# A two-layer graph network on one core: PSUM groups are seeded from SBUF by ScalarE, and the identity's term of panels 2 to 7 moves from TensorE to VectorE

## What is computed

```python
# layer 0
d = rsqrt(sum(adj, axis=1) + 1e-6)
h0 = (d[:, None] * (adj + eye(N)) * d[None, :]) @ (x @ W0)
x1 = layernorm(x + h0)
# layer 1
msg = relu((adj @ x1) @ W_msg.T + b_msg)
out = layernorm(x1 + gru_cell(msg, x1, W_ih, W_hh, b_ih, b_hh))
```

## Time and profile before

| | us |
|---|---|
| median of 3 runs (range) | 1829.5 (1828.28 to 1831.34) |
| the profiled execution, device time | 1829.18 |
| its span in the trace | 1827.4 |
| PE busy | 1677.5 (92%) |
| DVE busy | 1467.0 (80%) |
| ACT busy | 662.3 (36%) |
| POOL busy | 138.0 (8%) |
| mean granted TensorE clock | 0.992 |

### The profile page before, as it was taken

One profiled execution on the slowest core, in us unless ns is written; L12 is line 12 of the kernel. 1 busy time (PEld: TensorE's weight loads), 2 busy tenths in 40 slices (PEclk: granted clock), 3 DMA queues, 4 the chain that ended last, 5 costly groups with the idle time before them and its releaser, 6 DMA issues.

```text
span 1827.4 us, 16989 instructions
## 1 busy us (share of the span) xinstructions
PE 1677.5 (92%) x6496; PEld 1178.2 (64%) x6496; DVE 1467.0 (80%) x1380; ACT 662.3 (36%) x594; POOL 138.0 (8%) x110
## 2 busy tenths in 40 slices
PE   0088799996999999999999999999999999999996
PEld 0043254442544555888888888888788888888884
DVE  7888899999999974767666656665789898888886
ACT  0000000000000003544544444444576676766663
POOL 0000000000000001100000000000001112121212
PEclk9999999999999999999999999999999999999998
DMA  9999999999999962666666665665999999999991
GB/s 391 421 386 421 421 422 421 421 418 422 382 422 420 419 268 86 203 195 198 199 202 191 199 198 191 199 197 186 333 346 322 309 324 307 318 311 311 319 310 54
DMA packets 180929, 551.12 MB, mean 302 GB/s; under 512 B 13424, under 2 KB 13936, under 8 KB 148080
## 3 DMA queue, kind: packets, MB, share of 16 engines
q1 hardware_dynamic: 177280, 541.11, 80.5%
q0 software_dynamic: 2560, 8.39, 1.4%
q10 hardware_dynamic: 1008, 0.53, 0.1%
HBM read 545.79 MB, written 4.19 MB: 301 GB/s over the span
## 4 chain that ended last, share of the span: by engine, by line
PE 77%; DVE 12%; DMA 9%; issue 2%; ACT 1%; POOL 0%; SPq 0%; DVEq 0%; ACTq 0%; POOLq 0%
PE bank L501 17%; PE bank L503 17%; PE bank L502 17%; PE bank L449 16%; DMA ring<-adj_blocks 6%; DVE colsum L804 5%; DVE feat L808 2%; DVE feat L811 2%; DMA pool<-adj_blocks 2%; DMA kept<-adj_blocks 1%; PE bank L574 1%; PE bank L572 1%; PE bank L573 1%; PE bank L434 1%; PE bank L568 1%
## 5 line engine op out<-in xcount | busy, mean ns | idle before, releaser
L829 DVE TENSOR_TENSOR lo<-ring,hi 128x2048 fp32r<-128x2048 f32 x206 | 470.4, 2290 | 252.2 <-ACT f L681 209.2
L670 ACT ACTIVATE hi<-ring 128x2048 fp32r<-128x2048 f32 x206 | 395.4, 1919 | 370.6 <-DMA ring<-adj_blocks 267.4
L501 PE MATMUL bank<-hi,x1s 128*128 128x512 f32 x1024 | 408.9, 399 | 3.6 <-DVE lo L829 2.4
L503 PE MATMUL bank<-hi,x1s 128*128 128x512 f32 x1024 | 399.4, 390 | 0.0
L502 PE MATMUL bank<-lo,x1s 128*128 128x512 f32 x824 | 320.9, 389 | 0.0
L449 PE MATMUL bank<-kept,feat 128*128 128x512 f32 x600 | 267.9, 597 | 11.8 <-DMA kept<-adj_blocks 11.8
L501 PEld LDWEIGHTS bank<-hi,x1s 128*128 128x128 f32 x1024 | 192.4, 188 | 47.4 <-issue 3.6
L503 PEld LDWEIGHTS bank<-hi,x1s 128*128 128x128 f32 x1024 | 192.2, 188 | 41.0
L449 PEld LDWEIGHTS bank<-kept,feat 128*128 128x128 f32 x600 | 113.2, 191 | 155.8 <-issue 137.7
L804 DVE TENSOR_TENSOR colsum<-colsum,kept 128x2048 f32<-128x2048 f32 x81 | 185.6, 2291 | 10.1 <-DMA kept<-adj_blocks 8.4
L644 ACT ACTIVATE dege<-bank 128x8 f32<-128x8 f32 x8 | 1.4, 177 | 516.7 <-PE bank L434 516.7
(11 more groups left out here) (107 smaller groups left out, 1701.1 us busy)
## 6 DMA issues: line engine op xcount, KB each, us to landing
ring<-adj_blocks SPq DMA_DIRECT2D x412, 512.0 KB, 5.3
kept<-adj_blocks SPq DMA_DIRECT2D x126, 1024.0 KB, 12.2
ring<-adj_blocks SPq DMA_DIRECT2D x85, 1024.0 KB, 12.1
more<-adj_blocks SPq DMA_DIRECT2D x100, 512.0 KB, 6.1
pool<-adj_blocks SPq DMA_DIRECT2D x45, 1024.0 KB, 12.2
xt<-x_t SPq DMA_DIRECT2D x8, 512.0 KB, 12.1
xin<-x POOLq DMA_DIRECT2D x16, 256.0 KB, 3.3
out<-y POOLq DMA_DIRECT2D x16, 256.0 KB, 3.7
```

The costliest lines, as they stand in the source:

```text
L501: pe.matmul(acc[:, :], fh, ah, start=start and c == 0, stop=False, skip_group_check=True)
L503: mm = pe.matmul(acc[:, :], fl, ah, start=False, stop=stop and c == KC - 1, skip_group_check=True)
L670: ins = act.activation(hi[:, n % NHI], raw(slot_of2[n]), ACT.Copy)
L829: ins = dve.tensor_tensor(flat(low(n)), flat(raw(slot_of2[n])), flat(hi[:, n % NHI]).bitcast(f32), ALU.subtract)
```

## The change

Four things change in the first sweep and one in the second.

- **Groups 8 to 36 start from the sum so far.** When group g ends, ACT copies it to `part` (`leave`, every group but the last now), and then copies the old sum of the panel of group g+2 from `part` into the bank pair just left (`seed`). PE begins group g+2 when it is seeded and accumulates on it. DVE's `add_group` is gone; the last group's halves are copied by DVE instead of added (`half_out`).
- **The identity's term** stays on PE for panels 0 and 1 (`SELF_PANELS = 2`). For panels 2 to 7 DVE adds d * feat to x in row order (`own_step`, four instructions of 128x128 for each of 12 rows of 512), ahead of `row_step`.
- **The planner** has no adds to place, and EVICT is 1.1 where it was 0.56. The order of loads, of sums and of products is the same; 60 of the 256 loads, from the 107th on, take another slot, nearly all by exchanging slots with a load close by.
- `row_step` of those rows waits for `own_ready` in place of xin's arrival.

```diff
+    SELF_PANELS = 2
...
-    SUM, SUM_LOW, SUM_FIRST, FOLD, ADD = 0.92, 1.0, 0.8, 0.5, 0.52
-    PRODUCT, SELF, DEGREES, SUPPORT, FEATURE, EVICT, MARGIN = 1.38, 0.72, 0.68, 0.72, 1.9, 0.56, 0.8
+    SUM, SUM_LOW, SUM_FIRST, FOLD = 0.92, 1.0, 0.8, 0.5
+    PRODUCT, SELF, DEGREES, SUPPORT, FEATURE, EVICT = 1.38, 0.72, 0.68, 0.72, 1.9, 1.1
...
             def product(P, j):
-                if begins and g >= 2:
+                if begins and g >= NP:
+                    pe.wait_ge(seeded, g - NP + 1)
+                elif begins and g >= 2:
                     group_left(pe, g - 2)
-                if j == 4 * P:
+                self_term = j == 4 * P and P < SELF_PANELS
+                if self_term:
                     add_self(P, g, begins)
...
-                                       start=begins and u == 0 and j != 4 * P,
+                                       start=begins and g < NP and u == 0 and not self_term,
...
             last = NP - 1
-            add_self(last, group_of[(last, 4 * last)], False)
...
+            def leave(t):
+                g = group_of[t]
+                if groups[g][1][-1] != t or g == len(groups) - 1:
+                    return
+                R = groups[g][0]
+                act.wait_ge(prod_done, product_no[t])
                 for h in range(2):
                     i = 2 * R + h
                     ins = act.activation(part[:, i * W:(i + 1) * W], group_bank(g, h)[:, :], ACT.Copy)
                 ins.then_inc(evicted, 1)
+                if NP <= g + 2 < len(groups):
+                    seed(g + 2)
+
+            def seed(g):
+                R = groups[g][0]
+                act.wait_ge(evicted, g - 1)
+                for h in range(2):
+                    i = 2 * R + h
+                    ins = act.activation(group_bank(g, h)[:, :], part[:, i * W:(i + 1) * W], ACT.Copy)
+                ins.then_inc(seeded, 1)
...
             for P in range(NP):
+                for t in before_degrees[P]:
+                    leave(t)
                 feature(P)
-                for g in {0: range(0, NP - 1), 1: [NP - 1]}.get(P, []):
-                    evict(g)
+                for t in after_degrees[P] + burst[P]:
+                    leave(t)
...
-            def add_group(g):
-                R, units = groups[g]
-                dve.wait_ge(prod_done, product_no[units[-1]])
-                for h in range(2):
-                    rows = part[:, (2 * R + h) * W:(2 * R + h + 1) * W]
-                    ins = dve.tensor_tensor(rows, rows, group_bank(g, h)[:, :], ALU.add)
-                ins.then_inc(added, 1)
...
+            def own_step(i):
+                q = norm_no[i]
+                dve.wait_ge(xin_in[q % 2], (q // 2) * 16 + 16)
+                for c in range(KC):
+                    ins = dve.scalar_tensor_tensor(xin[:, q % 2, c, :], feat0[:, i * KC + c, :],
+                                                   dinv[:, i * KC + c:i * KC + c + 1], xin[:, q % 2, c, :],
+                                                   ALU.mult, ALU.add)
+                ins.then_inc(own_ready, 1)
...
             split_lo(0)
             split_lo(1)
-            add_half(1)
+            own_step(whole[1])
+            own_step(whole[0])
+            dve.wait_ge(evicted, len(groups) - 1)
+            half_out(1)
             row_step(whole[1])
-            add_half(0)
+            half_out(0)
...
                     tall_step(i)
+                    if i // 2 >= SELF_PANELS:
+                        own_step(i)
```

More of the change, by code:

```diff
@@ L127, in gnn_resnorm_kernel @@
             ready.append((max(now["dve"], landed[at_sum]), 1, "sum", at_sum))
-        ready += [(max(now["dve"], t), 0, "add", g) for g, t in ended_groups.items()]
         begin, _, kind, of = min(ready)
@@ L143, in gnn_resnorm_kernel @@
         elif kind == "product":
-            now["pe"] = multiplied[of] = begin + PRODUCT + (SELF if of[1] == 4 * of[0] else 0)
+            now["pe"] = multiplied[of] = begin + PRODUCT + (SELF if of[1] == 4 * of[0] and of[0] < SELF_PANELS else 0)
             g = group_of[of]
             if groups[g][1][-1] == of:
[L147 to L150, removed]
+                left[g] = now["pe"] + EVICT
         elif kind == "degrees":
@@ L165, in gnn_resnorm_kernel @@
                 to_fold = T1[of][0]
-        elif kind == "fold":
+        else:
             now["dve"] = folded[of] = begin + FOLD
             to_fold = None
[L169 to L172, removed]
     freed_at = {s: max(summed[m], multiplied.get(T1[m], 0)) for s, m in holder.items()}
@@ L370, in group_left @@
         def group_left(eng, g):
[L372 to L375, removed]
+            eng.wait_ge(evicted, g + 1)
         block = ctx.enter_context(nc.Block())
@@ L458, in add_self @@
                               feat0[:, P * WP // 128 + c, :], ident[:, :],
-                              start=begins and c % KC == 0, stop=False, skip_group_check=True)
+                              start=begins and g < NP and c % KC == 0, stop=False, skip_group_check=True)
             pe.wait_ge(consts, 2)
@@ L540, in turn @@
                 if i in whole:
-                    pe.wait_ge(last_added, q + 1)
+                    pe.wait_ge(last_out, q + 1)
                 else:
@@ L816, in _ @@
                         dve.tensor_tensor(csum, colsum[:, 0, :], colsum[:, 1, :], ALU.add).then_inc(csum_ready, 1)
-                    for g in range(NP, len(groups) - 1):
-                        if add_after[g] == n and n < NT1 - 1:
-                            add_group(g)
             dve.wait_ge(weights_in, NW * 16)
@@ L862, in row_step @@
                 dve.wait_ge(turned, q + 1)
-                dve.wait_ge(xin_in[q % 2], (q // 2) * 16 + 16)
+                if i // 2 < SELF_PANELS:
+                    dve.wait_ge(xin_in[q % 2], (q // 2) * 16 + 16)
+                else:
+                    dve.wait_ge(own_ready, q + 1)
                 for c in range(KC):
@@ L942, in out_step, with half_out @@
                     .then_inc(out_ready, 1)
-            def add_half(h):
+            def half_out(h):
                 g = len(groups) - 1
@@ L951, in add_half @@
                 rows = part[:, (2 * groups[g][0] + h) * W:(2 * groups[g][0] + h + 1) * W]
[L952 to L956, removed]
+                dve.tensor_copy(rows, group_bank(g, h)[:, :]).then_inc(last_out, 1)
             split_lo(0)
             split_lo(1)
-            add_half(1)
+            own_step(whole[1])
+            own_step(whole[0])
+            dve.wait_ge(evicted, len(groups) - 1)
+            half_out(1)
             row_step(whole[1])
-            add_half(0)
+            half_out(0)
             x1_step(whole[1])
```

16 lines of the change are left out of this document (6 added, 10 removed).

## The result

The changed kernel takes **1814.8 us** (median of 4 runs, 1813.56 to 1815.5), the kernel before 1829.0 in the same comparison: a ratio of 0.9917 with an interval of 0.9905 to 0.9929, 14.2 us less; the interval reaches from 12.9 to 17.4 us. One execution of the kernel warm (experiment 9) took 2656 us at a mean clock of 0.62 and is left out of its numbers. The profiled execution took 1815.5 us with a span of 1813.6, 13.8 us under the span of before, where 16.0 was forecast.

A forecast was written before the change was run, and what follows sets the result against it. PE was taken to bound the first sweep from panel 3's degrees (454.88 us) and the second sweep. Terms 3.66 + 3.42 + 8.90 = 16.0 us gave 1813.5 from 1829.5 us; 8-in-10 range 1810.5 to 1819.5.

The forecast's parts named there:

- term 1: At panel 3, with the adds off DVE, PE's wait for the closed row sum goes: 3.66 us.
- term 2: Behind panel 3's wait, the half-speed clock on the degrees and three products goes with the wait: 3.42 us.
- gaps of 1.3 us: PE's waits between loads before 450 us: they stay and do not lower the clock, which averages 0.97.
- term 3: Identity's matmuls of panels 3 to 7 leave PE in its bound 260 us: 5 x 1.78 = 8.90 us.
- panel 2's run is worth nothing: Panel 2's identity run lies where PE waits for loads; its gain is waited away before 447 us.
- Loads and sums keep ahead: First sweep behind panel 3: loads and DVE's sums arrive in time for a PE up to 16 us earlier.
- first rival: Clock falls all the same (1816.9 us) or blocks come late in stage 5 (1816.0 us); chance 0.26 for the two.
- ACT's seeds: ACT's copies into PSUM, taken as 0.6 us each, finish before PE needs the bank: cost 0.
- DVE's new steps: Second sweep: 12 rows of four small DVE instructions, 1.1 to 1.4 us a row, cost 0, at most 0.5.
- third rival: Second sweep: DVE's 12 new steps delay tiles' low parts and PE waits for each, 1827.1 us; chance 0.05.
- second sweep as a pure translation: The second sweep is PE's; what the first sweep gains or loses is handed on to the end.
- A dip of the clock elsewhere behind 451: Listed sign of a wrong forecast: PE's clock falling at another place after 451 us.

The follow-up runs named there:

- warm: Changed kernel plus 48 extra 128x128 identity matmuls on PE ahead of the first degrees, where PE waits for loads: 1813.98 us.
- experiment 9: Changed kernel plus 48 extra 128x128 identity matmuls on PE ahead of the first degrees (the kernel warm): 1813.98 us.
- experiment 2: Kernel before, adds still on DVE, with only the identity's term of panels 2 to 7 moved to DVE: 1821.7 us.
- experiments 2 and 3: Experiment 2, 1821.7 us, and the changed kernel with 30 chained small memsets on DVE ahead of panel 3's closing add, 1823.96 us.
- experiment 4, late_short: Changed kernel with 14 chained small memsets on DVE ahead of panel 3's closing add: 1816.62 us.
- experiment 1: Changed kernel with groups still seeded, but the identity's term of all 8 panels back on PE: 1822.76 us.
- experiment 7, slow_seed: Changed kernel with eight small copies on ACT ahead of each of the 29 seeds: 1814.21 us.
- after_again: The changed kernel itself, unedited, measured and profiled a second time: 1814.80 us.
- self_later: Changed kernel with panel 0's identity run moved from ahead of its burst to the head of the panel's last group: 1812.52 us.
- late_mid: Changed kernel with 20 chained small memsets on DVE ahead of panel 3's closing add: 1819.16 us.
- late_long: Changed kernel with 30 chained small memsets on DVE ahead of panel 3's closing add: 1823.96 us.
- self_again: Same code as self_later, run a second time beside the changed kernel on one chip: 1813.46 us.
- late_hidden: Changed kernel with 10 chained small memsets on DVE ahead of panel 3's closing add, leaving PE no wait there: 1813.52 us.

## Why the prediction was right

- **Adds off DVE, term 1 (3.66 us).** The closing add begins at 448.26, forecast 447.3; the block ahead of it, (3, 31), lands at 445.8 and is added from 445.94, so DVE's lag is 0.1 us where it was 6.3. The slots that 60 loads changed are not what took the lag away: the block landed at 445.0 before and lands at 445.8 now, so it is DVE that was late. No wait of PE. With the next point 7.08 us forecast, 7.14 in experiment 2.
- **The clock, term 2 (3.42).** 1.68 and 10.41 us for 3.58 and 11.93. Right, and experiments 2 and 3 bring the dip back together with the wait. The reason that I gave for the gaps of 1.3 us holds as far as it goes: they stand in the trace after too, as the bracket at 448.44 shows, and the windows of 10 us from 420 to 460 keep a clock of 1.00. But experiment 4 shows that it was nearer than I thought: 0.87 us of waiting for the sum, 3.7 us of work behind such a gap, brought the fall. By the Trainium skill, "TensorE: Matmul & The Clock Gate", section "HAM oscillation — how this bites in real kernels", waits for DMA of some 3 to 5 us between short pieces of matmul work bring the low clock. The trace agrees for the wait of 3.66 us, and goes further with that of 0.87. The prediction left the length of these waits out: the gaps of 1.3 us are no case of that section, so the trace doesn't disagree with it there, and the section wouldn't have made term 2 nothing.
- **Identity off PE, term 3 (8.90).** 8.95 in experiment 1, 8.28 at the first turn and 0.67 for that run's earlier start. That panel 2's run is worth nothing agrees with this: a sixth run would have made it 10.7.
- **Loads and sums keep ahead.** DMA moves 419, 421 and 424 GB/s in the three windows of 10 us from 460 on. DVE's closing add for panel 5 begins at 590.92 and is over at 592.2, where 591.3 was forecast, and PE comes at 596.42; no PE wait stands between 451 and the first turn. The first rival did not happen.
- **ACT's seeds (0).** 592 ns a copy, where I took 595, and no wait; doubled in experiment 7 without effect.
- **DVE's new steps (0 to 0.5).** 345 ns each, 13.5 us for 48, 1.13 us a row from start to end, of the 1.1 to 1.4 that I gave. The x1 of row 12 is ready at 741.00 + 0.69 = 741.69 and PE takes it at 742.76: the 1.1 us of slack are still there. The sweep keeps its 15.1 us up to the 105th tile, so the third rival is out. No run changes these steps alone within the changed kernel; this is read from the trace.

Two terms were missing from the sum. The start, -0.9, is no part of the change, and a profile with the same start (after_again) has 16.2 us at the first turn. The 105th tile, -1.3, I had not looked at: I took the second sweep as a pure translation, while it has a wait of 2.4 us in which little decides whether the clock falls. "A dip of the clock elsewhere behind 451" was a sign of being wrong in the prediction, and it came, for 1.3 us and not the 3.4 of its rival, at a place that the prediction had not weighed. Over these kernels waits of 1.5 and 1.6 us leave it up; one of 1.9 brings it down in self_later and another leaves it up in late_mid; 2.37 leaves it up in before, 2.36 brings it down in late_long. So the wait's length alone doesn't decide, and not the code alone either, as self_later and self_again show. late_hidden (1.5 and 1.2 us) and slow_seed (1.5, 0.2 and 0.6) have more and shorter waits and no fall, and end 1.3 and 0.6 us under the changed kernel although both do more work. What sets the wait there stays open. The chain of waits runs from a load through ACT's high part to DVE's low part; I made no kernel that changes it.

## What to carry to other kernels

When an engine that feeds PE's sequence is late, look for the clock behind the wait as well: at panel 3, with gaps of 1.3 us ahead, waits of 0.9 to 5 us cost 1.8 to 4.8 us of clock. It is no law: at the 105th tile waits of 1.3 to 1.6 us cost none in six profiles. Work moved off the bound engine was worth its time in the stretch where that engine is bound (8.95 us for 8.90), and panel 2's share, in the stretch before it where PE waits for loads, nothing. Where loads set the pace for hundreds of microseconds, look at the first hole in the DMA's work: one run of 8 small matmuls (16 records) taken from ahead of a burst to a later group put the first turn 0.8 and 2.3 us earlier in two profiles.

## What the runs showed of the hardware

- A copy by ACT into PSUM costs what one out of PSUM costs (592 and 595 ns for 128x512 f32), and PE accumulates onto it without a step in between.
- The clock can fall behind the work that follows a wait, and not at once: in late_short the degrees ran at full clock for 1.8 us, and the fall came within the product behind them (a clock of 0.50 from 456 to 458 us).
- The granted clock recorded while PE stands for 66 us, between the first support at 22 us and the first degrees at 92, differs between executions of one kernel (0.50 in the profile after, 1.00 in after_again). In both, the first degrees take 3.57 to 3.58 us, which is what those of panel 3 took at a recorded 0.50, so the recorded 1.00 is not the speed they ran at. The difference shows only in the identity's run at 106 us, 2.84 and 2.08 us. It was worth 1.1 us at the first turn.
- In the stretch where loads set the pace the clock can fall unseen. PE's timeline of the changed kernel has, where a longer wait comes behind one of 1.37 us,

```profile
407.41 3.67 PE L444 MATMUL bank<-pool,feat 128*128 128x512 f32 x8 [1.37 <-DMA pool<-adj_blocks]
413.56 5.40 PE L444 MATMUL bank<-kept,feat 128*128 128x512 f32 x8 [2.48 <-DMA kept<-adj_blocks]
418.79 3.60 PE L444 MATMUL bank<-ring,feat 128*128 128x512 f32 x8
```

5.40 us for a product of 3.67: the same 1.7 us as in late_short, but the next loads are waited for anyway (1.11 us ahead of the block at 423.50), so it need not cost anything at the end.
